# GpSimd's order of work in a transformer kernel's layer loop: the second norm's root moved ahead of the bias additions, and the norms' constant moved to VectorE

## The reference

```python
h = layernorm(x, ln1_s, ln1_b)
q, k, v = h @ Wq + bq, h @ Wk + bk, h @ Wv + bv   # 16 heads of 8
x = x + (linear_attention(q, k, v) @ Wo + bo)
h = layernorm(x, ln2_s, ln2_b)
x = x + relu(h @ W1 + b1) @ W2 + b2
```

## Time and profile before

| | us |
|---|---|
| median of 3 runs (lowest, highest) | 643.33 (642.86, 643.84) |
| the profiled execution | 647.06 |
| its span, first to last instruction | 645.2 |
| PE busy in the span | 568.3 (88%) |
| DVE busy | 422.9 (66%) |
| POOL busy | 327.9 (51%) |
| ACT busy | 250.7 (39%) |

### The profile page before, as it was taken

How to read it: one execution, slowest core, us unless ns; L and a number is a source line. 1 busy time by engine, 2 the same in 40 slices (tenths; PEclk the granted TensorE clock), 3 DMA queues, 4 the chain that set the end, 5 groups by cost and what they waited for, 6 DMA issues and landing times. The chain is left out here.

```text
span 645.2 us, 13057 instructions
## 1 busy us (share of the span) xinstructions
PE 568.3 (88%) x4715; PEld 475.4 (74%) x4715; DVE 422.9 (66%) x1278; ACT 250.7 (39%) x472; POOL 327.9 (51%) x365
## 2 busy tenths in 40 slices
PE   6988786669999999998998797999999999998881
PEld 4776663569999999998948684777776677775650
DVE  4579778993444444443338775687878787878783
ACT  3133247002333333332331325343444444446754
POOL 4863400887777777777641353344333343335331
PEclk9999899778999999999998988899999999999996
DMA  8990001125888998897259200000000100000001
GB/s 292 415 378 18 9 26 34 44 56 171 279 279 281 283 271 287 277 284 242 83 171 410 111 1 1 14 5 19 16 12 4 33 12 4 16 17 2 1 1 65
DMA packets 29568, 79.45 MB, mean 123 GB/s; under 512 B 7104, under 2 KB 12096, under 8 KB 29264
## 3 DMA queue, kind: packets, MB, share of 16 engines
q1 hardware_dynamic: 23088, 65.66, 29.9%
q0 software_dynamic: 6432, 13.16, 7.0%
HBM read 62.57 MB, written 16.25 MB: 122 GB/s over the span
## 5 line engine op out<-in xcount | busy, mean ns | idle before, releaser
L821 PE MATMUL bank<-hidden,ring 128*128 128x160 f32 x768 | 118.8, 306 | 1.4 <-DVE hidden L1863 1.4
L288 POOL TENSOR_SCALAR veps<-mv 128x4 f32<-128x4 f32 x52 | 15.7, 302 | 204.3 <-DVE mv L278 95.9
L821 PEld LDWEIGHTS bank<-hidden,ring 128*128 128x128 f32 x768 | 109.9, 195 | 1.8 <-DVE hidden L1863 1.8
L1875 DVE TENSOR_TENSOR hidden<-bank,hidden 128x480 f32<-128x480 f32 x64 | 42.1, 658 | 99.2 <-ACT hidden L1254 99.2
L1486 POOL DMA_INDIRECT returned_rows<-x1t,scatter_all x80 | 79.8, 998 | 27.8 <-issue 21.3
L1254 ACT ACTIVATE hidden<-bank 128x480 f32<-128x480 f32 x64 | 36.6, 571 | 91.2 <-PE bank L821 91.2
L1479 POOL DMA_INDIRECT arena<-dispatch_rows,gather_all x50 | 53.2, 1064 | 29.2 <-DVE scatter_all L1821 14.1
L1005 PE MATMUL bank<-ring,arena 128*128 128x128 f32 x512 | 65.2, 283 | 1.4 <-issue 1.4
L1005 PEld LDWEIGHTS bank<-ring,arena 128*128 128x128 f32 x512 | 61.0, 196 | 3.6 <-issue 2.4
L831 PE MATMUL bank<-hidden,ring 128*128 128x160 f32 x384 | 63.0, 300 | 0.5 <-DVE hidden L1875 0.5
L1319 ACT ACTIVATE arena<-bank,layer_cols 128x512 f32<-128x512 f32 x64 | 43.7, 687 | 38.3 <-PE bank L995 38.3
(11 more groups left out here) (235 smaller groups left out, 1085.0 us busy)
## 6 DMA issues: line engine op xcount, KB each, us to landing
ring<-in_ew SPq DMA_DIRECT2D x64, 576.0 KB, 5.2
returned_rows<-zeros SPq DMA_DIRECT2D x16, 512.0 KB, 14.9
arena<-returned_rows SPq DMA_DIRECT2D x6, 512.0 KB, 12.6
hidden<-returned_rows SPq DMA_DIRECT2D x4, 512.0 KB, 6.2
ring<-returned_rows SPq DMA_DIRECT2D x4, 512.0 KB, 9.6
ring<-in_l1w SPq DMA_DIRECT2D x8, 256.0 KB, 2.7
returned_rows<-x1t,scatter_all POOLq DMA_INDIRECT x80
shared<-in_xr SPq DMA_DIRECT2D x1, 1024.0 KB, 8.1
```

The lines of the kernel that those rows point to most:

```text
L821: mm = pe.matmul(bank[2 * (n % 2) + part][:, CAP * f:CAP * f + CAP], ring[:, n % RING, P * (FB * part + f):P * (FB * part + f) + P], E["xt ...
L1875: v.tensor_tensor(E["prod"][:, n % 2, :], bank[2 * (n % 2)][:, 0:FB * CAP], E["silu"][:, n % 2, :], ALU.mult).then_inc(sem("prod_g_ready"), 1)
```

## The change

It has four parts. Behind the aggregates VectorE makes `veps`, for all norms, and counts every aggregate in its Chain; GpSimd's `norm_rstd` is the power alone. GpSimd's Chain, the loop arithmetic for it and the semaphore steps go away. In GpSimd's slot the root of norm2 comes first; `add_bo` waits for `apply_norm2` and `add_b2` for the query features of the slot. `scale_final` loses a wait for its own engine's norm.

```diff
@@ norm_stats, norm_rstd
             v.sem_inc(sem("steps"))
-            var_ready = sem(f"var{NORMS[kind][0]}_ready")
+            for i in range(GT):
+                k = ch.did(v.bn_aggr(mv[:, s, i, :], stats[:, s, i, :]))
+            ch.after(k)
             if shifted or kind in ("first", "second", "last"):
-                for i in range(GT):
-                    k = ch.did(v.bn_aggr(mv[:, s, i, :], stats[:, s, i, :]))
-                ch.after(k)
-                v.tensor_scalar(neg_mean[:, s, :], mv[:, s, :, 0], -1.0, None, ALU.mult).then_inc(var_ready, 1)
-            else:
-                for i in range(GT):
-                    ins = v.bn_aggr(mv[:, s, i, :], stats[:, s, i, :])
-                ins.then_inc(var_ready, 1)
-
-        pool_steps = Chain(None, sem("pool_step"))
+                v.tensor_scalar(neg_mean[:, s, :], mv[:, s, :, 0], -1.0, None, ALU.mult)
+            v.tensor_scalar(veps[:, s, :], mv[:, s, :, 1], EPS_LN, None, ALU.add).then_inc(
+                sem(f"var{NORMS[kind][0]}_ready"), 1)
...
             pool.wait_ge(sem(f"var{which}_ready"), before + n + 1)
-            pool.sem_inc(sem("steps"))
-            pool_steps.after(pool_steps.did(pool.tensor_scalar(veps[:, s, :], mv[:, s, :, 1], EPS_LN, None, ALU.add)))
             pool.tensor_tensor(rstd[:, s, :], veps[:, s, :], minus_half[:], ALU.pow).then_inc(
@@ GpSimd's slot
             def slot(t, k, l):
                 g = k % GROUPS
+                norm_rstd(pool, "norm2", t - 2, g - 2)
+                pool.wait_ge(sem("h2_ready"), t - 1)
                 add_bo(t, g, layer_of(l, k, 0))
+                pool.wait_ge(sem("q1_ready"), t + 1)
                 add_b2(t - 2, (g - 2) % GROUPS, layer_of(l, k, 2))
-                norm_rstd(pool, "norm2", t - 2, g - 2)
                 if item(k, -1):
                     norm_rstd(pool, "norm1", t + 1, g + 1)
@@ GpSimd's pipeline
-            def body(l):
-                if l is None:
-                    pool_steps.end_loop(LAYERS - 1)
-                else:
-                    pool_steps.loop(l - 1, 2 * GROUPS)
-
-            pipeline(pool, fill, slot, tail, body)
+            pipeline(pool, fill, slot, tail)
@@ VectorE: scale_final, and the steps of one layer
-                v.wait_ge(sem("var0_ready"), NORMS["final"][1] + g + 1)
...
-            steps = GROUPS * (2 * GT + 1 + 3)
+            steps = GROUPS * (2 * 2 * GT + 1 + 3)
```

More of the change, by code:

```diff
@@ L1433, in _ @@
             pool.memset(minus_one[:], -1.0).then_inc(sem("minus_one_ready"), 1)
-            pool_steps.eng = pool
-            pool_steps.did(pool.memset(new_token[:], 1.0))
-            pool_steps.after(pool_steps.did(pool.memset(minus_half[:], -0.5)))
+            pool.memset(new_token[:], 1.0).then_inc(sem("pool_consts"), 1)
+            pool.memset(minus_half[:], -0.5).then_inc(sem("pool_consts"), 1)
+            pool.wait_ge(sem("pool_consts"), 2)
             pool.memset(new_token[:].rearrange("p (i e) -> p i e", e=NE)[:, :, 0:1], 0.0).then_inc(
```

## The result

| | before | after |
|---|---|---|
| median of 22 runs each (lowest, highest), us | 642.9 (639.41, 647.45) | 639.47 (637.19, 642.96) |
| profiled execution, us | 647.06 | 640.55 |
| its span | 645.2 | 638.7 |

The ratio is 0.9949 with an interval of [0.9934, 0.9964]: 3.3 us faster, between 2.3 and 4.2. Forecast were 1.5 us, so the sign was right and the size less than half of it.

A forecast was written before the change was run, and what follows sets the result against it. TensorE's 5.3 us of waits for apply_norm1, behind GpSimd's rstd, were taken to cap the loop's gain. Loop -1.1, tail -0.6, fill and first stage +0.2 make -1.5 us: 643.33 to 641.8 us, range 640.0 to 643.7.

The forecast's parts named there:

- what bounds the loop: Layer loop: TensorE's 12 waits of 0.4 us for apply_norm1, behind GpSimd's rstd; 12 x 0.09 = 1.1 us off.
- The hold of the power by the key features: Loop, norm1: rstd is held beside features_k and ends 0.89 us behind it, at A+1.68 (A: aggregates' end) against A+1.77.
- The start: Loop, norm1: with VectorE making veps, rstd may start at A+0.40, A being the end of the aggregates.
- no cost for the order and the additions: GpSimd's loop slot: norm2's root first gains nothing, since slack follows; the later bias additions cost nothing.
- Fill, first stage and tail: Outside the loop: tail 0.6 us off (0 to 1.0), fill and first stage 0.2 on (0.2 off to 0.5 on).
- The link: Outside the loop, where neg_mean is made: rstd comes 0.31 us earlier less 0.08 for the new instruction, 0.23.
- The sign ahead of the loop: First stage and fill: VectorE's new instruction costs TensorE 3 x 0.08, fill about as often; 0.2 us on in all.
- TensorE's wait of the earlier trace: Tail: TensorE's 0.40 us wait for apply_norm2 of the last group but one, worth 0 to 0.40, taken as 0.2.
- Not held: Loop rival, 10%: rstd ends at A+1.44 (A: aggregates' end), each slot loses 0.33 us, 638.9 us in all.
- The rivals with a longer hold: Loop: the hold eats the gain (22%, 643.3 to 643.6 us), or the port passes to residual1 (6%, 649.1 us).
- residual1 as the holder: Loop rival, 6%: L2045 also keeps rstd out, 0.52 us late in 12 slots, 6.2 us slower, 649.1 us.
- the low end: Whole kernel: lower bound of the range, 640.0 us, or 640.3 in the forecast's own range.

The follow-up runs named there:

- e1: Kernel before with only the order of GpSimd's slot and its two waits changed, GpSimd still adding the constant: 642.27 us, ratio 0.9997.
- e4: Changed kernel without the two new waits in GpSimd's slot: 639.5 us, ratio 0.9946.
- e3: Changed kernel with residual1 ahead of the key features in VectorE's slot: 637.02 us, ratio 0.9907.
- e5: Changed kernel with the step semaphore's increment put back between GpSimd's wait and the power: 640.1 us in one run.
- e2: Changed kernel with GpSimd's old order, bias additions first, keeping VectorE's constant: 638.79 us, ratio 0.9937.

## Why the prediction was too small

**Right: what bounds the loop, and by how much.** -1.1 us was forecast and -1.2 came. The hold of the power by the key features has the size that the earlier trace rows gave (0.89 behind the two-input instruction there, 0.88 here), and the 0.09 us a slot are 0.10. The start was forecast wrongly, A+0.40 instead of A+0.29, with no effect: a held power ends where the holder lets it. The rule of the Trainium skill (SBUF — State Buffer, "Who interferes with whom"), taken literally, has the power run whole behind the key features, which would end it at A+1.83; the runs show A+1.68, so the prediction was right to weigh higher.

**Right: no cost for the order and the additions.** e1 and e4 show both to lie in slack, as the text argued from the earlier trace rows.

**Wrong: the step "Fill, first stage and tail".** It put +0.2 us on fill and first stage and -0.6 on the tail. Measured by the stages: first stage -0.7, fill -0.35, tail -1.1, of which 0.37 is the pause, which I had not seen. So of the 1.9 us between the sum of -1.5 and the stages' -3.4 about 1.3 lie ahead of the loop, 0.4 are the pause, and the rest of the tail and the loop make up the small remainder. Three terms of the step failed:

- *The link.* It was costed at 0.23 us (0.31 less 0.08) with a hand-over of 0.20. Without GpSimd's own instruction ahead of the power the hand-over is 0.08, so that an unheld link gives 0.35. In the fill it is seen by itself: apply_norm2's wait for rstd is 1.58 us in the earlier trace rows and 1.13 after; less the 0.08 that VectorE spends, that is 0.37.
- *The sign ahead of the loop.* I counted there what VectorE's new instruction costs TensorE, 3 x 0.08 from the earlier trace rows, and a rstd or two given back. The runs showed that VectorE itself is held by GpSimd's bias addition behind the power in two groups of the first stage, so that it gains 0.36 us in each where I had charged it 0.08. The duration of 1.54 us at L1626, where the same shape takes 0.68, stood in the trace of before; I had looked at the waits in this stage and not at long durations, and a hold by the other engine is no wait in the profile.
- *TensorE's wait of the earlier trace rows.* Worth 0 to 0.40, I took 0.2; it went whole. The transpose in question now runs on from the one ahead of it without a wait (eight matmuls in one row), and the stretch of the tail that hangs on it, between the next two residual2, is 8.07 us instead of 8.49:

```profile
583.41 1.04 PE L893 MATMUL bank<-consts,arena 128*128 128x128 f32 x8
```

**The rivals.** Not held (10%) is not what happened, though the time came near it (639.47 against 638.9): e3 shows what the loop does when the power isn't held, 13.38 a slot. The rivals with a longer hold are excluded by the end at A+1.68 (the constant starts 0.04 behind the aggregates, not 0.15) and, for residual1 as the holder, by e3. Of the range the low end was too high: it took the upper bound of the tail, and of the stages ahead of the loop a gain of 0.2 at most. A further 0.4 us between the forecast of 641.8 and the 639.47 is the base: it was worked from 643.33, the median of three runs, where 22 give 642.9.

**Open.** Why the pause in the tail comes and goes with VectorE's program. And whether the stretches that scatter (start, experts, the rest of the fill) hold a few tenths more of either sign: the stages' 3.4 us agree with the ratio's 3.3, whose interval is wider than that.

## What to carry to other kernels

Look for instructions of one shape that take longer in some places than in others before pricing a change to a neighbouring engine: two engines that hold each other off show no wait, only a duration, and that is where a shorter chain on one of them gives time to the other. An instruction that is held ends a set time behind its holder (this power 0.87 to 0.89 us), so a shorter way to its start is worth nothing there and its whole length elsewhere. And where the executions of a kernel scatter by more than the change, compare fixed distances inside the profiles, one kernel for each part of the change.

## What was not expected of the hardware

- A semaphore increment of GpSimd's own between its wait and its next instruction costs 0.10 us: VectorE's end to GpSimd's start is 0.08 us without and 0.18 (e5) to 0.20 with it.
- A VectorE instruction of four columns and one input is held by a GpSimd addition of 512 columns: 1.07 us in e2, 1.28 in the tail of the changed kernel (beside the addition at 590.30), against 0.17 alone.

```profile
590.30 1.27 POOL L1520 TENSOR_TENSOR x1t<-shared,ring 128x512 f32<-128x512 f32 x1
590.32 1.28 DVE L275 TENSOR_SCALAR veps<-mv 128x4 f32<-128x4 f32 x1
```

- Part of the start of a GpSimd instruction gets done before it is held: the power started later in e5 by 0.10 us and was shorter by 0.11.
